# Count matrix of a graph kernel: row-sum pairs in turns of six lines, one table word per cell, source one-hots two ahead; and a 15-way search for the chosen nodes

## The reference

```python
x = _layernorm(x + _L0_gnn_ref(x, ...))      # mean of the neighbours
x = _layernorm(x + _L1_gnn_ref(x, edge_attr_128, ...))   # sums of edge rows over both ends, divided by counts
x = _layernorm(x + _L2_gnn_ref(x, ...))      # two attention layers
x = _layernorm(x + _L3_gnn_ref(x, ...))      # two mean layers, top-k, two mean layers
...
# inside _L3_gnn_ref
score = jax.nn.sigmoid(h @ w_score + b_score)[:, 0]
_, idx = jax.lax.top_k(score, k)             # k = N // 4, ties go to the lower node number
new_val = jnp.zeros((n, h.shape[1]), h.dtype).at[idx].set(h[idx])
```

## Time and profile before

| | |
|---|---|
| median of 3 runs | 8792.43 us (8791.13 to 8801.91) |
| profiled execution, its own time | 8789.98 us |
| its span | 8788.1 us |
| mean granted clock | 0.888 |
| stage b, first gather to the last line sent off | 1413.9 to 3056.6 us |
| search in stage e | 7798.75 to 7916.45 us |

### The profile page before, as it was taken

The page is one execution under the profiler, slowest core; times in us unless marked ns, Lnnn a source line. Parts: engine busy times, 40 slices in busy tenths (PEclk is TensorE's granted clock), DMA queues, the critical chain, the costliest instruction groups (busy, mean ns, idle before and its releaser), DMA issues. The chain is left out here.

```text
span 8788.1 us, 152768 instructions
## 1 busy us (share of the span) xinstructions
PE 6369.6 (72%) x40358; PEld 4395.3 (50%) x40359; DVE 4480.7 (51%) x12127; ACT 2215.2 (25%) x4744; POOL 3403.5 (39%) x3460
## 2 busy tenths in 40 slices
PE   0366602666666669999976777767777599959999
PEld 0255501444443335555546767667776355535555
DVE  6877754656666622222227777777777401131111
ACT  1221201333334410100004555435555100000000
POOL 0777776666664100000007777567777000000000
PEclk6678756888898879999989999989999799979999
DMA  0122201222223246676752222222222366636666
GB/s 16 45 71 71 67 3 47 92 85 86 86 93 83 67 124 174 182 186 170 189 135 54 54 55 55 47 57 54 53 55 55 94 191 189 189 87 177 192 191 182
DMA packets 871578, 901.11 MB, mean 103 GB/s; under 512 B 421539, under 2 KB 820226, under 8 KB 864867
## 3 DMA queue, kind: packets, MB, share of 16 engines
q1 hardware_dynamic: 753541, 637.16, 26.4%
q0 software_dynamic: 109664, 179.92, 9.4%
q10 hardware_dynamic: 8064, 80.29, 2.3%
HBM read 722.84 MB, written 93.87 MB: 93 GB/s over the span
## 5 line engine op out<-in xcount | busy, mean ns | idle before, releaser
L1919 POOL DMA_INDIRECT d_row_ring<-table_att,src_at x1664 | 1583.7, 952 | 644.8 <-issue 493.1
L2449 PE MATMUL psum<-e_a_ring,e_parts 128*128 128x448 bf16 x8232 | 1577.5, 353 | 83.6 <-DVE e_parts L2531 83.6
L2449 PEld LDWEIGHTS psum<-e_a_ring,e_parts 128*128 128x128 bf16 x8232 | 806.2, 98 | 824.2 <-issue 87.6
L775 POOL DMA_INDIRECT b_row_ring<-edge_attr,b_entry x896 | 892.3, 996 | 606.3 <-SPq L752 366.2
L794 PE MATMUL psum<-b_hot 128*128 x2920 | 672.6, 373 | 604.9 <-DVE b_hot L976 534.5
L353 POOL DMA_INDIRECT listed<-a_record,a_slot_no x832 | 867.7, 1043 | 315.0 <-issue 272.4
L1327 PE MATMUL psum<-c_a_ring,c_parts 128*128 128x448 bf16 x4116 | 812.8, 356 | 46.3 <-DMA c_a_ring<-adjacency 41.5
L1944 PE MATMUL psum<-edges_out,edges_in 128*128 128x120 f32 x4896 | 694.3, 301 | 157.9 <-ACT edges_in L2010 156.7
L794 PEld LDWEIGHTS psum<-b_hot 128*128 x2920 | 293.2, 100 | 959.0 <-issue 838.5
L1944 PEld LDWEIGHTS psum<-edges_out,edges_in 128*128 128x128 f32 x4896 | 644.0, 212 | 203.7 <-issue 203.7
L976 DVE TENSOR_SCALAR b_hot<-b_iota,b_key_dst 128x896 int16 (+1 forms) x1460 | 710.0, 486 | 2.1 <-issue 2.1
(11 more groups left out here) (427 smaller groups left out, 7939.8 us busy)
## 6 DMA issues: line engine op xcount, KB each, us to landing
e_a_ring<-adjacency SPq DMA_DIRECT2D x1372, 224.0 KB, 2.8
c_a_ring<-adjacency SPq DMA_DIRECT2D x686, 224.0 KB, 2.9
adjacency<-b_line ACTq DMA_DIRECT2D x49, 1568.0 KB
a_cum<-edge_attr SPq DMA_DIRECT2D x103, 512.0 KB
d_row_ring<-table_att,src_at POOLq DMA_INDIRECT x1664
b_row_ring<-edge_attr,b_entry POOLq DMA_INDIRECT x896
listed<-a_record,a_slot_no POOLq DMA_INDIRECT x832
e_a_left<-adjacency_left SPq DMA_DIRECT2D x28, 224.0 KB, 3.3
```

Source lines behind the costliest of these rows:

```text
L775: pool.indirect_dma_start(out=row_ring[:, u % 4, g, 0:D], out_offset=None, in_=a["edge_attr_128"], in_offset=bass.IndirectOffsetOnAxis(ap= ...
L1919: pool.indirect_dma_start(out=row_ring[:, u % 4, g, :], out_offset=None, in_=table_att[layer], in_offset=bass.IndirectOffsetOnAxis(ap=src_ ...
L2449: mm = nc.tensor.matmul(psum[:, 2 * (turn % 2) + v, 0:WIN], parts[:, piece, s, :], a_ring[:, s % SEVEN, v * WIN:(v + 1) * WIN], start=(s = ...
```

## The change

In stage b, the second and the third kind of line go: the lines run in eight turns of six, with TURN = (2, 2, 1, 2, 2, 1) twos, ten in all, and the last two follows. The loop body is thus six lines long on DVE and PE. One word of a table (`cell_row[0:1, 1]`) now holds a cell's first column, its number of fours and, shifted by 19, the number of fours before, so DVE's `befores` load goes; it is made by two operations more ahead of the loop. The source one-hots are made two twos ahead, so four stand before the first line instead of two. Adds and one-hots alternate (`turned_over`), and an add waits for the end of the one before it, ahead of itself. PE's order (two, cells 3 to 6, perhaps two, cells 0 to 2) and its own loads stay as they are.

In stage e a round tests up to 15 candidates at once: eight rounds for the score (3 candidates, then seven times 15), one for those above, and four for the node number (1, then three times 15). Compare and sum go over 15 x 49 elements a partition instead of 49, PE's product has 15 columns instead of one, and the ties are told by adding 2 NP to the node numbers of the others, once. The steps (`score_step`, `node_step`) are made when the stage begins, in 31 fills and 12 small operations. DVE's and PE's loops over rounds are written out.

```diff
-    MORE = TWOS - NT
+    TURN = (2, 2, 1, 2, 2, 1)
+    TURN_TWOS = sum(TURN)
...
+                with pe.Fori(0, NT // len(TURN)) as i:
+                    for k, twos in enumerate(TURN):
+                        s, m = i * len(TURN) + k, sum(TURN[:k])
+                        units = codes_of(pe, out_pairs, UNITS - 1, i * (2 * TURN_TWOS) + 2 * m, 2 * twos)
+                        before = befores(pe, i * (len(TURN) * NWIDE) + (k * NWIDE + 3), NWIDE + 1)
+                        two(i * TURN_TWOS + m, m % 2, units[0:2])
+                        cells(s, 3, NWIDE, before)
+                        if twos == 2:
+                            two(i * TURN_TWOS + (m + 1), (m + 1) % 2, units[2:4])
+                        cells(s + 1, 0, 3, before[NWIDE - 3:])
...
+                def add(i, h, code):
+                    at = bass.ds(code[0], 1)
+                    dve.wait_ge(s_sum, i * 2 + (h + 1))
+                    hold(dve, s_added, i * 2 + (h + 2), s_held_dve)
...
+                def turned_over(i, parity, pair, later):
+                    for h in range(2):
+                        add(i, h, pair[h])
+                        hot_of(parity, h, later[h])
...
+                with dve.Fori(0, NT // len(TURN)) as i:
+                    for k, twos in enumerate(TURN):
+                        s, m = i * len(TURN) + k, sum(TURN[:k])
+                        pairs = codes(i * (2 * TURN_TWOS) + 2 * m, 4 + 2 * twos)
+                        spans = spans_of(dve, i * (len(TURN) * NWIDE) + (k * NWIDE + 3), NWIDE)
+                        cells(s, 3, NWIDE, spans)
+                        if twos == 2:
+                            turned_over(i * TURN_TWOS + m, m % 2, pairs[0:2], pairs[4:6])
+                            m, pairs = m + 1, pairs[2:]
+                        cells(s + 1, 0, 3, spans[NWIDE - 3:])
+                        turned_over(i * TURN_TWOS + m, m % 2, pairs[0:2], pairs[4:6])
...
+        DIGITS = 15
+        SCORE_STEPS = [(28, 3), *((shift, DIGITS) for shift in range(24, -1, -4))]
+        NODE_STEPS = [(12, 1), (8, DIGITS), (4, DIGITS), (0, DIGITS)]
...
+                    for turn, (shift, n) in enumerate(SCORE_STEPS):
+                        st.by(V.tensor_tensor(cands[:, 0:n], score_step[:, turn, 0:n], thr[:].broadcast_to([P, n]), ALU.bitwise_or))
...
+                        st.by(V.tensor_tensor(beyond[:, 0:n, :], bc(score[:], 1, [P, n, NT]),
+                                              bc(cands[:, 0:n].bitcast(F32), 2, [P, n, NT]), ALU.is_ge))
                         st.settle(dve)
+                        st.by(V.tensor_reduce(hits[:, 0:n], beyond[:, 0:n, :], AX_X, ALU.add))
+                        counted(turn)
+                        st.by(V.tensor_scalar(passed[:, 0:n], psum[:, 7, 0:n], float(TOP), float(1 << shift), ALU.is_ge, ALU.mult))
                         st.settle(dve)
...
+                        st.by(V.tensor_reduce(kept_f[:], passed[:, 0:n], AX_X, ALU.add))
+                        st.settle(dve)
+                        st.by(V.tensor_copy(kept[:], kept_f[:]))
+                        st.settle(dve)
+                        st.by(V.tensor_tensor(thr[:], thr[:], kept[:], ALU.bitwise_or))
+                        st.settle(dve)
```

More of the change, by code:

```diff
@@ L713, in spans_of @@
             def spans_of(eng, q, n):
[L714 to L718, removed]
+                because = "a cell holds its first column, its number of four columns and how many came before"
+                words = cell_row[0:1, 1, q:q + n] if isinstance(q, int) else cell_row[0:1, 1, bass.ds(q, n)]
+                return [(nc.s_assert_within(eng.snap((code >> 9) & 1023), 0, COLS - 4, skip_runtime_bounds_check_because=because),
+                         nc.s_assert_within(eng.snap(code & 511), 1, COLS // 4, skip_runtime_bounds_check_because=because),
+                         eng.snap(code >> 19))
+                        for code in loaded(eng, words, 30)]
             def left_of(eng):
@@ L978, in cell, with cells @@
                             last.then_inc(s_hot, 1)
-                def cells(s, first, end, spans, before):
+                def cells(s, first, end, spans):
                     for w in range(first, end):
-                        cell(s, slice(w * WIDE, (w + 1) * WIDE), spans[w - first], before[w - first])
+                        cell(s, slice(w * WIDE, (w + 1) * WIDE), spans[w - first])
                 def codes(q, n):
                     return codes_of(dve, out_pairs, UNITS - 1, q, n)
[L987 to L1021, removed]
@@ L1022, in _, with hot_of @@
-                cells(NT - 1, 3, NWIDE, spans_of(dve, (NT - 1) * NWIDE + 3, NWIDE - 3),
-                      befores(dve, (NT - 1) * NWIDE + 3, NWIDE - 3))
-                adds(TWOS - 1, codes(2 * TWOS - 2, 2))
+                def hot_of(parity, h, code):
+                    tile, unit = code
+                    V.tensor_tensor(is_src[:, parity, h, :, :], bc(key_src[:, bass.ds(unit * G, G)], 2, [P, G, P]),
+                                    bc(iota[:, bass.ds(tile * P, P)], 1, [P, G, P]), ALU.is_equal).then_inc(s_is_src, 1)
@@ new lines, in _ @@
+                for i in range(2):
+                    for h, code in enumerate(codes(2 * i, 2)):
+                        hot_of(i, h, code)
+                cells(0, 0, 3, spans_of(dve, 0, 3))
+                with dve.Fori(0, NT // len(TURN)) as i:
[9 more added lines that the diff above has]
+                        turned_over(i * TURN_TWOS + m, m % 2, pairs[0:2], pairs[4:6])
@@ L1026, in _ @@
+                cells(NT - 1, 3, NWIDE, spans_of(dve, (NT - 1) * NWIDE + 3, NWIDE - 3))
+                for h, code in enumerate(codes(2 * TWOS - 2, 2)):
+                    add(TWOS - 1, h, code)
+                dve.wait_ge(s_added, 2 * TWOS + 2)
                 st.by(V.tensor_reduce(most[:], edges_out[:, 0:NT, D], AX_X, ALU.max))
@@ L2466, in _ @@
                         pe.wait_ge(s_prod_free, 2 * (turn + 1))
[L2467 removed]
+                        for i in range(SEARCH):
                             pe.wait_ge(s_count, 2 * i + 1)
[L2469 removed]
+                            nc.tensor.matmul(psum[:, 7, 0:DIGITS], ones[:], hits[:], start=True, stop=True).then_inc(s_count, 1)
                 finish(len(PASSES) - 1)
```

119 lines of the change are left out of this document (57 added, 62 removed).

## The result

The changed kernel takes 8659.42 us in the median of four runs (8652.77 to 8667.18), the kernel before 8791.78 (8787.13 to 8801.91): 0.9847, interval 0.9834 to 0.9859, or 132 us less. The forecast was 285 us less, and 8659 lies above its range. The sign was right, the search's term was right, and stage b's was three times too large.

The account below looks back on a forecast made before the run. The prediction took the gather chain to bound stage b's first loop and, after the change, its end. From 8790.0 us it took 211 for stage b and 74 for the search: 8505, median 8507, range 8465 to 8600.

Parts of the forecast that it names:

- 107 x 12.4 = 1327 us: Stage b, gather chain from unit 4 to unit 111 at 12.4 us a unit, before 18 us for bursts.
- lands 12.2 us later, PE multiplies its last two and half a line of cells follows: End of stage b: from unit 111's start at 2816 us to line 48 leaving at 2845 us.
- the second rival: Stage b: the gather collides more with other transfers, 12.9 us a unit, unit 111 54 us later, 8561 us; chance 0.10.
- Rival 1: Stage b: DVE and PE hinder each other through `hot`, lines stay at 29.5 to 31 us, 8560 to 8612; chance 0.20.
- The gather is slower, so it sets the end: Stage b after the change: the gather's 28.6 us a line, not DVE's 26.5, decides when line 48 leaves.
- Lines 1 to 3 did more in 29.2: Stage b, argument against the first rival: early lines with two twos and seven fours each took 29.2 us.
- DVE's pace: Stage b after the change: DVE needs 26.5 us a line, 48 of them 1272 us.
- The cover: Stage b: PE's loads and two run while DVE turns over and loads; only a loss over 2.1 us a line shows.
- The stream of code: Stage b loops: the six-line body's branch back costs DVE 3.6 us once in six lines, 0.6 us a line.
- the third rival: Stage b: every small loop refetches its code, 343 cells x 3.6 us, result near 9650 us; chance 0.03.
- The fourth: Stage b: the shares do nothing, only the search's 74 us is gained, 8718 us; chance 0.03.
- The search: Stage e: the search takes 44 us instead of 117.7, 74 us less, with 62 to 83 allowed for.

Follow-up runs that it names:

- two_go: The changed kernel with SP letting a second unit go before it waits for the first: 8596.49 us, 0.9789 of the kernel before.
- b_only: The kernel before with only stage b's change and the old search, on the other kind of chip: 11312.85 us, 1.0024 of the kernel before.
- search_only: The kernel before with only the 15-way search and the old stage b, on the other kind of chip: 11208.79 us, 0.9931 of the kernel before.
- pe_load4: The changed kernel with one more unused eight-word table load on PE in each line, last repeat, other kind of chip: 0.9952 of the kernel before.
- old_loops_two_go_search: The kernel before with only SP letting two units go and the 15-way search: 0.9735 on the usual kind of chip, 1.0134 and 1.0101 on the other.

## Why the prediction was wrong, and where right

- **Which step failed.** The mechanism held: the gather's chain with SP's gap set the pace. Two of its terms were too small, and they are the whole of stage b's miss. First, "107 x 12.4 = 1327 us", with 18 for bursts 1345, from unit 4 to unit 111: it took 1424.5, 79.5 more. Second, what comes behind unit 111's start, "lands 12.2 us later, PE multiplies its last two and half a line of cells follows", 29 us: it took 2989.3 - 2896.8 = 92.5, 63.5 more. With 0.8 us of a later unit 4 that is the 144 us between the forecast 2845 and 2989.3.
- **Why the chain was longer.** The eight gathers kept their length (10.09 us, 10.05 before). The gap behind them was 3.22 us instead of 2.32, since landings came late. A landing is told to SP 1.7 us behind the last gather's end in the median; it took 4.5 us on average for the 14 units whose last gather began within 4 us after a line was sent off, and 2.0 for the 87 others up to unit 105 (before: 3.0 for 14, 1.7 for 87). So the gather collides with the writing of the lines, which is the second rival's mechanism; it was given 12.9 us a unit and a chance of 0.10, and 13.31 were measured. That it is the collision is read from this coincidence and wasn't tested. The landings of units 107 to 110 took 6.0 to 9.2 us, in the kernel before 5.9 to 9.0, where PE did not have to wait for them; why they are slow isn't shown.
- **Why the end was longer.** The forecast lets unit 111 belong to the last two. PE waits for it at the first of the last four twos (pairs 154 to 161 of 0 to 161; the seven pairs behind 154 bring no later unit). Behind its landing at 2912.6 PE has those four twos and the cells of two and a half lines left, 76.7 us instead of 16.8. Just ahead of it, pairs 151 to 154 each wait for a unit of their own; at four pairs a line PE asks for four such units in some 31 us, where the gather brings one in 13 or more, and line 46 alone takes 52.0 us.
- **A third step, which this kernel hides in part.** Rival 1, where I wrote that PE's 20.2 us of busy time a line, "0.67 more of 5.2 and its own loads (2 to 3) make 26". I added busy time, and left out the time in which PE's sequencer prepares the next matmul. PE's stream is 29.8; table loads are 2.2 of it and branches back 0.54. "The gather is slower, so it sets the end" compared 28.6 with 26.5 and 26; with 29.8 PE would have been the slower one, and two_go shows where it would have stopped the gain: 1448.9 us from line 0 to line 48, 86 more than my 1363. A gather as quick as forecast would therefore have missed the forecast too.
- **The rival's size.** The trace is the first rival's in sign and nearly in size, 31.35 us a line against 29.5 to 31, but by luck. DVE and PE hindering each other through `hot` isn't what happened: PE waits for `hot` some 2 us in the stage. And the sign that I had set for this rival, POOL's waits well over 2.3 with DVE issuing all along, was there (3.2 us) and meant another thing: it doesn't tell late landings from a full ring. The end, 8659 against its 8612, is later by 36 us of the stage (0.75 us in 48 lines) and 2.7 of a later line 0; the rest is the difference of the unchanged stages.
- **"Lines 1 to 3 did more in 29.2"**, my argument against it, was no argument against PE's 29.8: it was nearly the same number, and PE was as likely as DVE to be what took it (by the records of those three lines, PE's stream is 29.1 and DVE's 29.1).
- **DVE's pace.** 27.6 for 26.5: I took 1.1 us a line too little. The waits of the adds for themselves went as told (0.4 us, once, for 34.0); its loads became two a line; the stand after its first branch back, up to 1644.55 us, was 5.16 us with two loads in it, where the 8.20 held three. DVE is not the bound, so the 1.1 us cost nothing here.
- **"The cover."** I said that PE's loads and two lie behind DVE's turning over, and that only a loss over 2.1 us a line shows. The cover didn't hold, DVE waits for PE 178.3 us in the stage; but as the gather was slower still, that cost nothing in the changed kernel. It shows in two_go.
- **The stream of code.** I took 3.6 us once in six lines for DVE, and nothing for PE. Both stand, and PE's is the one nearer the bound: 3.64 us in the median of its row, seven times. The Trainium skill, Runtime: NRT & Kernel Launch, "Instruction fetch mechanics", says that a taken branch to code outside the blocks held makes the engine stand; this trace agrees for PE (216 ns back over one or two lines, 3640 over six), and the small loops of the cells don't refetch (branches of line 966 on DVE: at most 80 ns), so the third rival is out. The fourth is too, as stage b gave 67 us.
- **The search.** Right: 43.0 us for 44. A round of 15 for the score takes 7756.73 - 7753.10 = 3.63 us (3.72 told), for the node 3.57 (3.57), the first 2.45 (2.5). Compare and sum take 0.93 and 0.92 us, so neither the quicker nor the slower case that I had allowed for came.
- **What is open:** why so many landings are late, and whether keeping the lines' writes apart from the gathers would bring them back; the direct cost of one more load on PE or DVE on the usual kind of chip. What stands for the gather as the bound is that SP waited for landings alone, that PE stood waiting for the last units, and that taking SP's gap away made the kernel 54 us faster and moved SP's waits to PE.

## What to carry to other kernels

To say which engine sets the pace, compare streams, not busy times: the stage's time less what an engine waits for others, its loads, address arithmetic and branches included. In two_go PE was the bound while busy for 69% of the stage. Where an engine that only keeps the books ends a wait, as SP does for POOL, ask what that engine waited for: the same row of POOL's waits meant landings in one kernel and PE in the other. For the end of a stage, look up where in the order of work the last unit is used, since all that lies behind it comes on top. Before work is spread to fit a slow producer, look whether its slowness is a wait in somebody's bookkeeping: letting two units go instead of one gave 148 us in the kernel before, and made the spreading worthless.

## What the runs showed of the hardware

The four chips of the other kind take 28 to 29% longer for the same kernel before. The granted clock in stage b is 0.77 in b_only there and 0.90 in the changed kernel on the usual kind, and in stage b, in the traces of these runs, the sequencers' own instructions pause. Line 966, DVE's register work in `cell` (ns, min/median/max), in b_only there:

```profile
L966 DVEq ALU_OP  x730: 3/45/1325, 2281.7 to 4329.6; - x183
...
L966 DVEq COMPARE_BRANCH  x365: 3/43/711, 2281.8 to 4329.6; - x183
```

and in the changed kernel on the usual kind:

```profile
L966 DVEq ALU_OP  x730: 40/45/50, 1457.4 to 3060.9; - x183
...
L966 DVEq COMPARE_BRANCH  x365: 43/43/80, 1457.5 to 3061.0; - x183
```

The medians are the same, and the longest are 1325 and 711 ns against 50 and 80. In b_only's stage b, 349 register instructions on DVE and 368 on PE take 0.4 us or more over their median, 0.64 and 0.66 in the median; in the changed kernel on the usual kind none does. 289 of DVE's 349 overlap a gather of POOL, though a gather runs for only 45% of the time; in search_only and pe_load4 it is 225 of 286 and 300 of 363. From 2 us after the last gather on there are none, and lines 46 and 47 are as quick as on the usual kind, 29.4 and 30.6 us, where the stage's mean is 40.4. The last gather, and lines 45 to 47:

```profile
4162.01 0.94 POOL L777 DMA_INDIRECT b_row_ring<-edge_attr,b_entry  x1 [0.30 <-issue]
...
4168.92 0.34 ACTq L867 DMA_DIRECT2D adjacency<-b_line  x1
...
4198.27 0.35 ACTq L867 DMA_DIRECT2D adjacency<-b_line  x1
...
4228.88 0.35 ACTq L867 DMA_DIRECT2D adjacency<-b_line  x1
```

There the order of the versions turns round: old_loops_two_go_search, the fastest on the usual kind at 0.9735, is at 1.0134 and 1.0101. What makes these chips so isn't known from these runs; that the pauses come with gathers in flight is seen in three traces, and wasn't tested by itself.
